# Ranking the edges over 5 columns at a time with running totals in PSUM, in a four-layer graph network on one core

## The reference

```
x = layernorm(x + L0(x, weight, edge_weight1, src, dst, edge_type_20))
x = layernorm(x + L1(x, W, M, src, dst))
x = layernorm(x + L2(x, ..., node_type_4, edge_type_8, src, dst))
x = layernorm(x + L3(x, edge_index, W, b, resW, resb))
```

```
h_all = jnp.einsum('ni,rio->nro', h, weight)        # 20 relations per node
msg = h_all[edge_src, rel_type] * norm
agg = jax.ops.segment_sum(msg, edge_dst, num_segments=h.shape[0])
return jax.nn.relu(agg)
```

## Time and profile before

| what | value |
| --- | --- |
| median of 3 runs | 4641.0 us (4636.3 to 4641.19) |
| the profiled execution | 4640.62 us |
| its span, first to last instruction | 4638.8 us |
| PE busy in the span | 3368.1 us, 73% |
| DVE busy | 2266.2 us, 49% |
| POOL busy | 1745.5 us, 38% |
| ACT busy | 1135.5 us, 24% |
| mean granted clock of TensorE | 0.744 of full speed |
| the first stage | from 0 to about 899.6 us |

### The profile page before, as it was taken

The page is one execution under the profiler, slowest core; times in us unless marked ns, Lnnn a source line. Parts: engine busy times, 40 slices in busy tenths (PEclk is TensorE's granted clock), DMA queues, the critical chain, the costliest instruction groups (busy, mean ns, idle before and its releaser), DMA issues. The chain is left out here.

```text
span 4638.8 us, 56452 instructions
## 1 busy us (share of the span) xinstructions
PE 3368.1 (73%) x12011; PEld 2226.8 (48%) x12011; DVE 2266.2 (49%) x6807; ACT 1135.5 (24%) x2963; POOL 1745.5 (38%) x1709
## 2 busy tenths in 40 slices
PE   4972228666666777776997957777767777789999
PEld 1430003355555211113884425666656566656887
DVE  9972000255555555554563436565545555574122
ACT  1320003100000233333102412333344444342121
POOL 2887770166655000002012356555535555500000
PEclk9985558777777655555998976666556666689999
DMA  4320003333322111111566764444424443415555
GB/s 133 144 104 26 26 26 125 113 87 88 88 82 81 43 69 66 69 67 49 157 192 222 294 233 129 117 121 122 120 80 124 124 124 118 117 36 174 181 203 179
DMA packets 224889, 539.65 MB, mean 116 GB/s; under 512 B 57972, under 2 KB 82710, under 8 KB 210902
## 3 DMA queue, kind: packets, MB, share of 16 engines
q1 hardware_dynamic: 112210, 257.22, 16.2%
q0 software_dynamic: 80224, 221.15, 15.5%
q10 hardware_dynamic: 32164, 57.91, 4.0%
HBM read 358.90 MB, written 177.22 MB: 116 GB/s over the span
## 5 line engine op out<-in xcount | busy, mean ns | idle before, releaser
L386 PE MATMUL ps<-w,xt 128*128 128x512 f32 x1000 | 472.4, 632 | 327.1 <-issue 224.7
L1093 PE MATMUL ps<-cells_wide,cells_near 128*128 128x448 bf16 x980 | 453.5, 566 | 149.5 <-issue 80.8
L334 POOL DMA_INDIRECT records<-rec,slots x391 | 481.0, 1230 | 203.8 <-issue 126.5
L1507 PE MATMUL ps<-q,onehot_t 128*128 x880 | 392.1, 592 | 219.9 <-DVE onehot_t L1608 128.4
L685 POOL DMA_INDIRECT rel_g<-table,rows_i x391 | 371.2, 949 | 430.2 <-POOLq L575 209.7
L685 POOL DMA_INDIRECT score_g<-table8v,rows_i x391 | 380.0, 972 | 336.8 <-SPq L697 231.0
L386 PEld LDWEIGHTS ps<-w,xt 128*128 128x128 f32 x1000 | 197.3, 201 | 585.3 <-issue 474.4
L685 POOL DMA_INDIRECT score_g<-table8k,rows_i x391 | 371.6, 950 | 274.9 <-SPq L697 163.0
L1743 PE MATMUL ps<-vx,score_onehot 128*128 128x261 f32 x880 | 382.9, 579 | 96.2 <-issue 46.3
L955 PE MATMUL ps<-rel_g,rel_onehot 128*128 x880 | 307.6, 484 | 192.8 <-DVE rel_onehot L978 127.5
L1507 PEld LDWEIGHTS ps<-q,onehot_t 128*128 128x128 f32 x880 | 234.7, 294 | 270.5 <-issue 237.8
(11 more groups left out here) (387 smaller groups left out, 5540.3 us busy)
## 6 DMA issues: line engine op xcount, KB each, us to landing
gcn_cells<-cells SPq DMA_DIRECT2D x250, 320.0 KB, 3.6
table<-tb SPq DMA_DIRECT2D x50, 1280.0 KB
conv_cells<-cells SPq DMA_DIRECT2D x125, 320.0 KB, 3.1
cells<-cells_kept SPq DMA_DIRECT2D x75, 448.0 KB, 2.5
score_dst_bc<-dst_rows ACTq DMA_DIRECT2D x110, 256.0 KB
sum_dst_bc<-dst_rows ACTq DMA_DIRECT2D x110, 256.0 KB
cells<-cells_kept SPq DMA_DIRECT2D x25, 256.0 KB, 2.0
records<-rec,slots POOLq DMA_INDIRECT x391
```

The source lines that it names most:

```text
L334: pool.indirect_dma_start(out=m.records, out_offset=bass.IndirectOffsetOnAxis(ap=slots[:, j:j + 1], axis=0), in_=rec[:, j, :], in_offset=N ...
L386: mm = pe.matmul(bank(m, g % 6, 0, 512), xt[:, k, :], w20[:, k, g * 512:(g + 1) * 512], start=(k == 0), stop=(k == 1))
L1093: mm = pe.matmul(out, near[:, i % HOTS, :], wide[:, i % HOTS, k * HALF:(k + 1) * HALF], start=False, stop=True, skip_group_check=True)
L1507: mm = pe.matmul(bank(m, i % UNROLL, j * D, (j + 1) * D), onehot_t[:, i % 2, j * P:(j + 1) * P], q, start=True, stop=True)
```

## The change

The number of columns of a part, SORT_COLS, goes from 33 to 5, and the parts, SORT_PARTS, from 12 to 79. `least` and `count`, 101 x 5 = 505 floats, move from SBUF to PSUM banks 5 and 7. The table of relations, which used banks 0 to 5, uses banks 0 to 4 (BANKS20), and PE may run five groups ahead of ACT. The function `place(h)` is split: `rank(h)` does scan, copy, multiplication and sum for 5 columns, and `place(first, last)` the six short instructions for all the columns of several parts. POOL is told of new columns ten times, after the parts in SORT_STOPS: after 10, 25, 50, 90, 140, 190, 240, 290, 340 and 391 columns, where it was twelve times, every 33. The scan takes the running value as the maximum of itself and `least`, then adds `onehot`, so that no extra column is needed. The product goes to a new tile `own`, with the keys innermost, so that the sum reads neighbours. POOL no longer clears `least`; DVE does, in PSUM. Some small tiles that lay inside `least` and `count` get room of their own.

```diff
-SORT_PARTS = 12
+SORT_COLS = 5
+SORT_STOPS = (2, 5, 10, 18, 28, 38, 48, 58, 68, 79)
...
-        key = sb("key", [P, SORT_PARTS, SORT_COLS + 1], BF16)
-        onehot = sb("onehot", [P, SORT_PARTS, KEYS, SORT_COLS + 1], U8)
-        least = sb("least", [P, KEYS, SORT_COLS + 1])
-        count = sb("count", [P, KEYS, SORT_COLS + 1])
+        key = sb("key", [P, SORT_PARTS, SORT_COLS], BF16)
+        onehot = sb("onehot", [P, SORT_PARTS, KEYS, SORT_COLS], U8)
+        least = bank(m, 5, 0, KEYS * SORT_COLS).rearrange("p (b j) -> p b j", b=KEYS)
+        count = bank(m, 7, 0, KEYS * SORT_COLS).rearrange("p (b j) -> p b j", b=KEYS)
+        own = sb("own_rank", [P, SORT_COLS, KEYS])
...
-            nc.gpsimd.memset(least[:, :, :], 0.0).then_inc(weighed, 1)
             nc.gpsimd.memset(rec[:, :, :], 0.0).then_inc(rec_zero, 1)
             pool.wait_ge(rec_ready, 5)
+            starts = (0,) + tuple(stop * SORT_COLS for stop in SORT_STOPS[:-1])
             for j in range(EJ):
-                if j % SORT_COLS == 0:
-                    pool.wait_ge(slots_ready, j // SORT_COLS + 1)
+                if j in starts:
+                    pool.wait_ge(slots_ready, starts.index(j) + 1)
...
-                    if g >= 6:
-                        pe.wait_ge(emptied, t * GROUPS20 + g - 5)
+                    if g >= BANKS20:
+                        pe.wait_ge(emptied, t * GROUPS20 + g - BANKS20 + 1)
...
-            def place(h):
-                lo, hi = h * SORT_COLS, min(EJ, (h + 1) * SORT_COLS)
-                step(nc.vector.tensor_tensor_scan(flat(count[:, :, :]), flat(onehot[:, h, :, :]), flat(least[:, :, :]), 0.0,
-                                                  ALU.add, ALU.max))
+            def rank(h):
+                step(nc.vector.tensor_tensor_scan(flat(count), flat(least), flat(onehot[:, h, :, :]), 0.0, ALU.max, ALU.add))
                 if h + 1 < SORT_PARTS:
-                    step(nc.vector.tensor_copy(least[:, :, 0], count[:, :, SORT_COLS]))
-                step(nc.vector.tensor_tensor(flat(count[:, :, :]), flat(count[:, :, :]), flat(onehot[:, h, :, :]), ALU.mult))
-                step(nc.vector.tensor_reduce(summed[:, h % 2, :], count[:, :, :].rearrange("p b j -> p j b"), AX.X, ALU.add))
...
+                    step(nc.vector.tensor_copy(least[:, :, 0], count[:, :, SORT_COLS - 1]))
+                step(nc.vector.tensor_tensor(own[:, :, :].rearrange("p j b -> p b j"), count, onehot[:, h, :, :], ALU.mult))
+                step(nc.vector.tensor_reduce(summed[:, h * SORT_COLS:(h + 1) * SORT_COLS], own[:, :, :], AX.X, ALU.add))
+
+            def place(first, last):
+                lo, hi = first * SORT_COLS, min(EJ, last * SORT_COLS)
+                step(nc.vector.tensor_scalar(pos_i[:, lo:hi], summed[:, lo:hi], -1.0, None, ALU.add))
...
-            dve.wait_ge(weighed, 1)
+            step(nc.vector.memset(least, 0.0))
             step(nc.vector.tensor_tensor(least[:, :, 0], sm(3), bank(m, 7, 0, KEYS), ALU.add))
-            place(0)
+            for h in range(SORT_STOPS[0]):
+                rank(h)
+            place(0, SORT_STOPS[0])
...
-            for h in range(1, SORT_PARTS):
-                place(h)
+            for first, last in zip(SORT_STOPS, SORT_STOPS[1:]):
+                for h in range(first, last):
+                    rank(h)
+                place(first, last)
```

More of the change, by code:

```diff
@@ L67 @@
 ACCW = D + HEADS + 1
-SORT_COLS = -(-EJ // SORT_PARTS)
+SORT_PARTS = -(-EJ // SORT_COLS)
+assert SORT_STOPS[-1] == SORT_PARTS
 CELL_ITEMS = USED + CELLS - 1
@@ L243, in sort_and_relation_table @@
         key_f = sb("key_f", [P, EJ])
-        key = sb("key", [P, SORT_PARTS, SORT_COLS + 1], BF16)
-        onehot = sb("onehot", [P, SORT_PARTS, KEYS, SORT_COLS + 1], U8)
-        least = sb("least", [P, KEYS, SORT_COLS + 1])
-        count = sb("count", [P, KEYS, SORT_COLS + 1])
-        free = least[:, :, :].rearrange("p b j -> p (b j)")
+        key = sb("key", [P, SORT_PARTS, SORT_COLS], BF16)
[3 more added lines that the diff above has]
+        own = sb("own_rank", [P, SORT_COLS, KEYS])
+        free = sb("tables", [P, 2 * CELL_ITEMS + 4 * ITEMS + 6 * (KEYS + 1)])
         late, many = free[:, 0:CELL_ITEMS], free[:, CELL_ITEMS:2 * CELL_ITEMS]
@@ L254, in sort_and_relation_table @@
         cell_f = free[0:1, o:o + 6 * (KEYS + 1)].rearrange("p (k i) -> p k i", k=6)
-        cell_n_items = count[0:1, :, :].rearrange("p b j -> p (b j)")[:, 0:CELL_ITEMS].bitcast(I32)
-        summed = sb("summed", [P, 2, SORT_COLS + 1])
+        cell_n_items = sb("cell_n_items", [1, CELL_ITEMS], I32)
+        summed = sb("summed", [P, SORT_PARTS * SORT_COLS])
         small = sb("small", [P, 5, KEYS + 1])
@@ L264, in sort_and_relation_table @@
         rec = sb("rec", [P, EJ, REC])
-        pos_i = sb("pos_i", [P, 2, SORT_COLS], I32)
-        lane_i = sb("lane_i", [P, 2, SORT_COLS], I32)
-        lane = sb("lane", [P, 2, 2, SORT_COLS])
+        pos_i = sb("pos_i", [P, EJ], I32)
+        lane_i = sb("lane_i", [P, EJ], I32)
+        lane = sb("lane", [P, 2, EJ])
         slots = sb("slots", [P, EJ], I32)
@@ L273, in sort_and_relation_table @@
         tb = sb("tb0", [P, 2, half])
-        (inputs, edges_in, x_in, x_zero, w_in, chain, counted, totals, weighed, placed, slots_ready,
+        (inputs, edges_in, x_in, x_zero, w_in, chain, counted, totals, slots_ready,
          rec_zero, rec_ready, xs_ready, turned, xt_ready, product, emptied, based, columned, spread_cells) = sems(
             ctx, nc, "sort", "inputs", "edges_in", "x_in", "x_zero", "w_in", "chain", "counted",
-            "totals", "weighed", "placed", "slots_ready", "rec_zero", "rec_ready",
+            "totals", "slots_ready", "rec_zero", "rec_ready",
             "xs_ready", "turned", "xt_ready", "product", "emptied", "based", "columned", "spread_cells")
@@ L282, in sort_and_relation_table @@
         stored = sems(ctx, nc, "sort", "stored0", "stored1")
-        m.spent += (inputs, edges_in, x_in, x_zero, w_in, chain, counted, totals, weighed, placed, slots_ready,
+        m.spent += (inputs, edges_in, x_in, x_zero, w_in, chain, counted, totals, slots_ready,
                       rec_zero, rec_ready, xs_ready, turned, xt_ready, product, emptied, based, columned, spread_cells,
@@ L288, in sort_and_relation_table @@
         HG = GROUPS20 // 2
+        BANKS20 = 5
         table = m.table20.rearrange("(n r) d -> n (r d)", r=RELS20)
@@ L385, in node_tile @@
                     for k in (0, 1):
-                        mm = pe.matmul(bank(m, g % 6, 0, 512), xt[:, k, :], w20[:, k, g * 512:(g + 1) * 512],
+                        mm = pe.matmul(bank(m, g % BANKS20, 0, 512), xt[:, k, :], w20[:, k, g * 512:(g + 1) * 512],
                                        start=(k == 0), stop=(k == 1))
@@ L442, in place @@
                 if h + 1 < SORT_PARTS:
-                    step(nc.vector.tensor_copy(least[:, :, 0], count[:, :, SORT_COLS]))
-                step(nc.vector.tensor_tensor(flat(count[:, :, :]), flat(count[:, :, :]), flat(onehot[:, h, :, :]), ALU.mult))
-                step(nc.vector.tensor_reduce(summed[:, h % 2, :], count[:, :, :].rearrange("p b j -> p j b"), AX.X, ALU.add))
-                n, k = hi - lo, h % 2
-                step(nc.vector.tensor_scalar(pos_i[:, k, 0:n], summed[:, k, 1:1 + n], -1.0, None, ALU.add))
@@ new lines, in rank @@
+                step(nc.vector.tensor_tensor(own[:, :, :].rearrange("p j b -> p b j"), count, onehot[:, h, :, :], ALU.mult))
[3 more added lines that the diff above has]
+                step(nc.vector.tensor_scalar(pos_i[:, lo:hi], summed[:, lo:hi], -1.0, None, ALU.add))
+                nc.vector.tensor_single_scalar(lane_i[:, lo:hi], pos_i[:, lo:hi], P - 1, op=ALU.bitwise_and)
+                step(nc.vector.tensor_single_scalar(key_i[:, lo:hi], pos_i[:, lo:hi], 7, op=ALU.logical_shift_right))
+                nc.vector.tensor_copy(lane[:, 0, lo:hi], lane_i[:, lo:hi])
+                step(nc.vector.tensor_copy(lane[:, 1, lo:hi], key_i[:, lo:hi]))
+                nc.vector.scalar_tensor_tensor(slots[:, lo:hi], lane[:, 0, lo:hi], float(USED), lane[:, 1, lo:hi],
```

11 lines of the change are left out of this document (2 added, 9 removed).

## The result

The changed kernel takes 4720.4 us (median of 4 runs, 4713.5 to 4735.5) where the kernel before takes 4638.7 us (4628.7 to 4641.2) beside it: the ratio is 1.0185, with a 95% interval of 1.0154 to 1.0215. So it is slower, by some 82 us. The profiled execution took 4724.8 us, with a span of 4722.7 us; the span of before was 4638.8, so 83.9 us are to be found.

The account below looks back on a forecast made before the run. The relation table bounds the first stage, PE being starved while POOL streams scatters unheld: 488 us of this for 407, 81 more x 0.844 = 68 us later. 4640.6 + 68 = 4709 us; range 4610 to 4755 (0.83).

Parts of the forecast that it names:

- POOL streaming unheld: First stage: unheld scatters slow PE and DVE to 1.40 us per instruction; table ends at 527 us plus 0.844 per us.
- The hold gone: DVE's scan and product, reading one SBUF and one PSUM tensor, no longer lengthen POOL's scatters (6.97 and 3.82 us before).
- Rival A: Scan and product from PSUM hold POOL as before; time within 5 us of 4641; chance 0.06.
- D: Rival: the slowing of PE and DVE isn't POOL's doing; table ends at 527, time about 4330; chance 0.05.
- the crawl of the first two streams: POOL's first two runs of scatters, before its long one: 20 us each of slowed PE and DVE.
- the crawl sets in at 90: PE and DVE slow to 1.40 us per instruction from 90 us, with POOL streaming from 74.
- the third stop: DVE's third release of columns to POOL: ready at 115 us; POOL waits up to 9 us and the queue drains.
- The second bound of the prediction: POOL's stream never breaks and lasts 391 x 1.313 = 513 us: +90 us.
- lies in time that it waits anyway: POOL's clearing of `least` before the first scatter goes; it falls within POOL's waiting, so its removal gains nothing.
- B, the chopped crawl,: Rival: the queue fills more slowly or drains at each stop; 4605 us, up to 4665 with partial drains; chance 0.11.
- C: Rival: new DVE forms hold scatters a little, to every 1.6 us, so PE isn't starved until 316; 4564 us; chance 0.07.
- E: Rival: POOL's stream is unbroken at 1.40 us per scatter; 4760 us; chance 0.05.

Follow-up runs that it names:

- experiment 1: POOL memset of 128x128 floats and a wait behind each scatter: kernel after 4388.8 us (0.947 of before), kernel before 4500.7 us (0.971).
- experiment 4: Kernel after with a smaller memset and wait behind each scatter: 4601.6 us (0.992) with 8 columns, 4426.3 us (0.954) with 64.
- experiment 2: Kernel after with `least` and `count` in SBUF again, still 5 columns a part: 4538.1 us, ratio 0.979.
- experiment 5: Kernel after with a second scatter of only 32 records behind each, into a tensor nobody reads: 5197.1 us, ratio 1.120.
- experiments 1 and 3: Kernel before with a 128x128 memset and wait behind each scatter, 4500.7 us; kernel before with the table in PSUM banks 0 to 4, 4637.6 us.

## Why the prediction was right, and what in it was off

**What bounds the stage, and the sign: right, and shown.** The prediction put the slowdown down to POOL streaming unheld, for 0.844 us of lost table per us. The pauses of experiments 1 and 4, the hold given back in 2 and the doubled stream in 5 all move the table's end. At POOL's own pace the rule gives its place: 523.3 + 0.844 x (520 - 7.5) = 956 for the kernel after, where 959.5 was measured, and 523.3 + 0.844 x 294 = 771 for experiment 2, whose scatters are unheld from 337.5 to 631.6 us, where 775.0 was measured. With a pause it doesn't hold, as experiment 4 shows.

**The hold gone: right**, from the one row beside L1615: 0.96 us per scatter, and 1.73 for every second one where the tensors are in SBUF again. Rival A is out. **D is out** by experiment 1, though its number, about 4330, wasn't far from what a paced kernel takes.

**The sum was 68, the table's end moved by 88.9.** The mis-sized term is the crawl of the first two streams, put at 20 us each. 436 us were lost (959.5 - 523.3), which is 517 us of crawl, where the prediction had 20 + 20 + 448 = 488. Those 29 us are 24.5 us of time. The step that failed is "the crawl sets in at 90" for all engines at once, 16 us after the stream begins. For PE it was about right (91 to 99 us). DVE was not slowed before 115.5, 44 us into the stream:

```profile
114.54 0.27 DVE L443 COPY ps<-ps 128x101 f32<-128x101 f32 x1
115.52 1.07 DVE L444 TENSOR_TENSOR own_rank<-ps,onehot 128x505 f32<-128x505 f32 x1 [0.71 <-DVE ps L443]
```

So the third stop (POOL's columns 25 to 49) was ready at 99.9, before POOL came to it at about 103, and not at 115. Only the fourth cost a wait, of 6.5 us for the 7 that had been reckoned, and one gap of 7.5 us hardly broke the crawl. The second bound of the prediction, +90 for an unbroken stream, was the better value. 68 + 24.5 is 92.5; the table's end moved by less, since the stage also began earlier.

**The stage's start: 4.1 us earlier (its first tile at 60.75 for 64.87), where 1 had been reckoned.** The one-hot instructions are 0.012 us closer together (0.485 for 0.497), which is the 1.2 us put down. Most of the rest came from the clearing of `least`, which the prediction had called a thing of no cost. In the kernel before, POOL clears `least` and then, from 6.17 us, `rec`; DVE's first instruction on the keys begins beside that and takes 2.73 us. The first row is of POOL, the second of DVE, in the kernel before:

```profile
6.17 2.70 POOL L326 MEMSET rec<- 128x3128 f32 x1
```

```profile
6.36 2.73 DVE L423 TENSOR_SCALAR key_i<-dst_i 128x391 int32<-128x391 int32 x1 [2.23 <-DMA src_i<-in_src]
```

and the same two in the kernel after:

```profile
3.28 2.71 POOL L329 MEMSET rec<- 128x3128 f32 x1 [0.63 <-POOLq L2494]
```

```profile
6.33 0.36 DVE L427 TENSOR_SCALAR key_i<-dst_i 128x391 int32<-128x391 int32 x1 [2.20 <-DMA src_i<-in_src]
```

POOL is done with `rec` at 5.99, before DVE begins, and the instruction takes 0.36. That is 2.4 us. In experiments 1 and 3, where the kernel before still clears `least`, it takes 2.71 and 2.66; no run took the clearing away alone. So POOL's work that "lies in time that it waits anyway" was on the path of another engine. The last 0.4 us are the conversion of the keys, one instruction where there were two. So 68 + 24.5 - 4.1 = 88.4 for 88.9 measured, and the 5.0 us by which the rest of the program was shorter leave 83.9. That the forecast, 4709, lies within 16 us of the profiled 4724.8 is in part luck: 24.5 us too few of crawl stand against 9 us that weren't in the sum.

**Smaller terms.** The part was put at 3.0 us and takes 3.37: the product with one operand in PSUM takes 1.07 us, not the 0.69 of L1615. Its output here is written by key and column from a byte operand, and from SBUF it takes 1.09, so it isn't PSUM's cost; which of the two it is, no run shows. It did no harm, since DVE wasn't last. In the crawl a part takes 5.6 us for the 5.5 reckoned, because there instructions are paced and their length doesn't matter. POOL's start at 71.3 for 74, 1.32 us per scatter for 1.31, the banks and SP at nothing: as put.

**B, the chopped crawl,** didn't come about at this rate; experiment 4 shows it where the scatters are 1.41 us apart, cut by POOL's own gaps and not by its waits for DVE. **C** came true where its condition was made, in experiment 2: 4538 us for the 4564 worked out. **E**, every scatter at 1.40, holds only from 410.7 us on, where the mean is 1.40.

**What the prediction didn't see** is that its sign belongs to a kind of chip. The trace of before came from one where the crawl exists. Nothing in it could tell that there are others where the same program is 740 us shorter and this change gains 2.8%.

## What to carry to other kernels

Where one engine issues small indirect DMAs back to back, look at what the others do beside it, not at its own busy share: short instructions spaced evenly at 1.40 us with nothing that releases them are the sign. Then an edit that frees that engine can lengthen the program, and a pause of 0.2 us per DMA, as long as another engine has the longer way to go, can be worth more than the edit. Time such an edit on more than one chip, and keep the pause only for those where the sign shows.

## What the runs showed of the hardware

- Indirect DMAs issued every 1.27 us on one kind of chip make each PE instruction cost 1.40 us (a tile of the table 117.6 us for 18.4), and each chained DVE instruction as well, later. PE is late after 17 to 20 us of the stream, fully starved after 27, and recovers 28 us after its last DMA; DVE after 44. At one per 1.41 us the crawl is milder and comes in pieces; at one per 1.465 there is nothing of it. A pause of 96 columns, 1.435 us, was only run on the other kind of chip, so the point isn't known closer.
- It goes by DMAs, not by records: 32 in place of 128 starve PE as much.
- Once such a stream is 26 to 27 us ahead of one DMA per 1.40 us, POOL is itself held to 1.40 us each (from 582.7 us in the kernel before, 410.7 in the kernel after, 255.4 in experiment 5).
- On a second kind of chip, with the same program, the same 0.96 us per scatter and the same quick tiles, there is no such effect, and 81 gathers go in 100 us where 68 went. What the engines and the DMAs share, and why the chips differ, no run here shows.
- Two tensors in SBUF as operands of a scan and a product hold one scatter in two from 0.96 to 1.72 us; with `least` and `count` in PSUM 388 of 391 scatters take 1.21 us or less, and DVE takes the same 3.4 us either way.
